# One-core transformer block with two expert mixtures: first mixture computed from held weights, first routing reordered

## What is computed

```python
y = attention(x, bias, mask, ...)            # 16 heads of 64, layer norms before and after
# first mixture: one expert of 8 for each token, at most ceil(T / 8 * 1.25) tokens to an expert, the others go to expert 0
final_e = _route(tokens, router_w)           # rank inside the expert by probability, ties by order
h = relu(tokens @ W1[e] + b1[e])             # 256 -> 1024
y = h @ W2[e] + b2[e]                        # 1024 -> 256
x = x + y
# second mixture: two experts of 8 for each token, and a shared part; then a gated layer of experts per sequence
x = x + gated(choice_mixture(x) + shared(x))
```

## Time and profile before

| | |
|---|---|
| median of 3 runs | 637.75 us |
| the profiled execution's own time | 638.58 us |
| its span, first to last instruction | 636.9 us |
| PE busy | 556.8 us, 87% of the span |
| DVE, ACT, GpSimd busy | 326.8, 247.3, 239.2 us |
| DMA | 80.05 MB, 126 GB/s mean |
| mean granted TensorE clock | 0.959 |

### The profile page before, as it was taken

One profiled execution on the slowest core, in us unless ns is written; L12 is line 12 of the kernel. 1 busy time (PEld: TensorE's weight loads), 2 busy tenths in 40 slices (PEclk: granted clock), 3 DMA queues, 4 the chain that ended last, 5 costly groups with the idle time before them and its releaser, 6 DMA issues.

```text
span 636.9 us, 11284 instructions
## 1 busy us (share of the span) xinstructions
PE 556.8 (87%) x3452; PEld 440.6 (69%) x3453; DVE 326.8 (51%) x973; ACT 247.3 (39%) x664; POOL 239.2 (38%) x392
## 2 busy tenths in 40 slices
PE   0599999662199999999999999999999989999895
PEld 0488888451056666666787897788888868777664
DVE  3477676459422222464253774444444425566665
ACT  0254454340022222222464433555565535444342
POOL 5322121000111112100482545565555427777860
PEclk9999999885599999999999999999999979999999
DMA  8940000039921101122347701565555623465662
GB/s 166 403 200 1 3 2 1 2 132 463 306 76 30 32 32 51 33 90 89 100 86 242 231 1 51 141 164 155 163 158 159 157 75 100 136 182 180 190 181 70
DMA packets 52222, 80.05 MB, mean 126 GB/s; under 512 B 11138, under 2 KB 43907, under 8 KB 51652
## 3 DMA queue, kind: packets, MB, share of 16 engines
q1 hardware_dynamic: 44004, 57.03, 26.1%
q0 software_dynamic: 8160, 22.29, 14.5%
HBM read 54.13 MB, written 25.17 MB: 125 GB/s over the span
## 4 chain that ended last, share of the span: by engine, by line
PE 76%; DVE 8%; DMA 4%; issue 4%; ACT 3%; POOL 3%; SPq 1%; another core or an unknown queue 0%; ACTq 0%; POOLq 0%; DVEq 0%
PE psum L1464 9%; PE psum L1383 9%; PE psum L1228 9%; PE psum L1246 8%; PE psum L1116 5%; PE psum L1478 5%; PE psum L1088 5%; PE psum L1393 4%; PE psum L1526 3%; PE psum L1456 3%; POOL arena L870 2%; PE psum L1238 2%; PE psum L1096 1%; PE psum L1411 1%; DMA arena<-x 1%
## 5 line engine op out<-in xcount | busy, mean ns | idle before, releaser
L870 POOL DMA_INDIRECT arena<-x,row_tok x72 | 69.3, 963 | 52.4 <-PE psum L1456 45.5
L870 POOL DMA_INDIRECT arena<-y_sorted,pos_k_i x64 | 63.7, 995 | 34.7 <-issue 15.3
L1464 PE MATMUL psum<-big_w,arena 128*128 x288 | 73.9, 379 | 0.0
L870 POOL DMA_INDIRECT arena<-h_late,row_tok x16 | 15.4, 960 | 145.6 <-PE psum L1220 84.8
L1383 PE MATMUL psum<-arena,big_w 128*128 128x256 f32 x256 | 62.5, 394 | 0.5 <-ACT arena L1816 0.5
L1526 PE MATMUL psum<-big_w,arena 128*128 x256 | 62.9, 379 | 0.0
L1228 PE MATMUL psum<-big_w,arena 128*128 x128 | 59.6, 609 | 0.8 <-DVE arena L2371 0.8
L1464 PEld LDWEIGHTS psum<-big_w,arena 128*128 128x128 f32 x288 | 54.5, 190 | 7.3
L1246 PE MATMUL psum<-arena 128*128 x256 | 58.0, 380 | 1.5 <-ACT arena L1729 1.5
L1383 PEld LDWEIGHTS psum<-arena,big_w 128*128 128x128 f32 x256 | 49.1, 199 | 8.5 <-ACT arena L1816 1.2
L1246 PEld LDWEIGHTS psum<-arena 128*128 128x128 f32 x256 | 47.5, 190 | 8.0 <-issue 2.2
(11 more groups left out here) (317 smaller groups left out, 1054.4 us busy)
## 6 DMA issues: line engine op xcount, KB each, us to landing
y_sorted<-arena SPq DMA_DIRECT2D x72, 128.0 KB
tokens<-x SPq DMA_DIRECT2D x4, 1024.0 KB, 22.2
x<-tokens SPq DMA_DIRECT2D x16, 256.0 KB, 3.0
z_kept<-arena SPq DMA_DIRECT2D x16, 256.0 KB
out<-arena SPq DMA_DIRECT2D x16, 256.0 KB
y_late<-arena SPq DMA_DIRECT2D x16, 128.0 KB, 1.7
big_w<-expert_w_t SPq DMA_DIRECT2D x1, 2048.0 KB, 8.1
arena<-x,row_tok POOLq DMA_INDIRECT x72
```

Source lines behind the costliest of these rows:

```text
L870: pool.indirect_dma_start(dst, None, rows, bass.IndirectOffsetOnAxis(ap=idx, axis=0)).then_inc(done, 16)
L1464: mm = pe.matmul(bank[2 + i % RT][:, 0:2 * M1], c_gt[i % RT][:, k, :], mgu_s[:, k, bass.ds(e, 1), :].rearrange("p a m -> p (a m)"), start= ...
```

## The change

Six edits:

- **Mixture.** `expert_up` holds W1 as the stationary operand (blocks of 128 x 128) and moves the 128 tokens: 16 matmuls of 128 columns whose result has the hidden units on the partitions. `turn_up`, `up_copy` and `act1` are gone; ACT's relu starts at half of expert_up (`up_half`), DVE's at its end; results and `act_t` alternate between two sets of buffers. The weights' place no longer depends on a register: tile i uses slot i mod 8 of `big_w`, and for tiles 8 to 15 SP loads the tile's W1 (1 MB, `load_w1`) when expert_up(i-8) is done. PE's loop is written out; it waits for the reloads before tiles 8 and 12.
- **Rows.** Seven tiles' variances, scaling and turning move ahead of the last projection on their engines; tile 7 alone follows it. The logits are computed in groups of 128 columns, the Exp table is loaded last.
- **Stores and loads.** SP stores seven tiles of `h_late` early, the last one apart. x is loaded after the table, the first gather and the two biases.
- **Comparisons.** ACT copies the spread keys to SBUF (`rows_s`), GpSimd makes "is less" for tiles 5, 6 and 7; tile 0's "is less or equal" is split in two.
- **Last tile.** DVE's relu of tile 15 precedes add_bias(14).
- **71 choice tiles** instead of 72; SP's store loop there is written out.

The diff, cut to its core (the general branch and plain renamings are left out):

```diff
-    TILES2 = -(-((2 * T + E1 * (P - 1)) // P) // RT) * RT
+    TILES2 = (2 * T + E1 * (P - 1)) // P
+act_t = [G.take(NF, P) for _ in range(2)]
+G.at += FF
...
+        sp.wait_ge(hnorm, NTW)
+        sp.dma_start(h_late[0:1, :], h_l[0:1, NTW, :]).then_inc(l_hs, 16)
+        sp.dma_start(late_rows[:, 0:NTW - 1, :], h_l[:, 0:NTW - 1, :]).then_inc(l_hs, 16)
         sp.wait_ge(hnorm, NTW + 1)
-        sp.dma_start(h_late[0:1, :], h_l[0:1, NTW, :]).then_inc(l_hs, 16)
-        sp.dma_start(h_late[1:, :].rearrange("(c p) d -> p c d", p=P), h_l[:, 0:NTW, :]).then_inc(l_hs, 16)
-        sp.wait_ge(l_ht, (NTW + 2) // 2)
-        sp.wait_ge(l_hs, 32)
+        sp.dma_start(late_rows[:, NTW - 1, :], h_l[:, NTW - 1, :]).then_inc(l_hs, 16)
         sp.dma_start(w2_s, w2.rearrange("p (e k d) -> p e k d", e=E0, k=NF)).then_inc(ld_w2, 16)
-        sp.wait_ge(l_lg, 1)
-        load_x()
     sp.wait_ge(table, 1)
     sp.wait_ge(got[0], 16)
     sp.dma_start(b1_s, b1).then_inc(ld_b, 16)
     sp.dma_start(b2_s, b2.rearrange("e d -> (e d)").partition_broadcast(P)
                  .rearrange("p (e d) -> p e d", e=E0)).then_inc(ld_b, 16)
+    load_x()
...
-        store_tile(0, 0)
-        with sp.Fori(0, E0 // 2 if late else (tiles - 1) // 2) as r:
-            for v in range(2):
+        def load_w1(i):
+            if i >= E0:
+                sp.wait_ge(up_ps, i - E0 + 1)
+            e = sp.value_load(tile_e[0:1, i:i + 1], min_val=0, max_val=E0 - 1)
+            sp.dma_start(w1_s[:, i % E0, :, :].rearrange("p k f -> p (k f)"),
+                         w1[:, bass.ds(e * (KD * FF), KD * FF)]).then_inc(w1_got[i // 4 % 2], 16)
...
+        for i in range(tiles - 1):
+            if i + E0 < tiles:
+                load_w1(i + E0)
+            store_tile(i, i % 2)
         sp.wait_ge(up_ps, tiles)
         load_shared()
...
+        pool.wait_ge(l_rows_ev, 2)
+        for m in range(NTW - NGB, NTW):
+            pool.tensor_scalar(beats[m][:, 0:(m + 1) * P], rows_s[:, 0:(m + 1) * P], key_l[:, m:m + 1], None, ALU.is_lt).then_inc(l_beat_g, 1)
...
             pe.wait_ge(l_beat, m + 1)
+            if m >= NTW - NGB:
+                pe.wait_ge(l_beat_g, m - NTW + NGB + 1)
...
-    def expert_up(i, e):
+    def expert_up(i):
+        u, at = i % 2, i % E0 * (KD * FF)
         pe.wait_ge(g_ev, i + 1)
-        pe.wait_ge(up_ev, i)
-        for k in range(KD):
-            for f in range(2):
-                mm = pe.matmul(bank[1 + f], g_t[:, k, :],
-                               big_w[:, bass.ds(e * (KD * FF) + (k * FF + f * 512), 512)],
+        if i >= 2:
+            pe.wait_ge(t_eva, i)
+            pe.wait_ge(t_evd, i)
+        for f in range(NF):
+            for k in range(KD):
+                c = at + k * FF + f * P
+                mm = pe.matmul(bank[1 + 2 * u + f // 4][:, (f % 4) * P:(f % 4 + 1) * P], big_w[:, c:c + P], g_t[:, k, :],
                                start=k == 0, stop=k == KD - 1)
+            if f == NF // 2 - 1:
+                mm.then_inc(up_half, 1)
         mm.then_inc(up_ps, 1)
...
-    def turn_up(j, u):
-        pe.wait_ge(up_ev, j + 1)
-        pe.wait_ge(t_eva, j + 1)
-        pe.wait_ge(t_evd, j + 1)
-        for f in range(NF):
-            mm = pe.transpose(bank[3 + f // 4][:, (f % 4) * P:(f % 4 + 1) * P], act1[u][:, f * P:(f + 1) * P], ident[:, :])
-        mm.then_inc(t_ps, 1)
...
-            mm = pe.matmul(bank[5 + u][:, 0:D], act_t[:, f, :], arena[:, bass.ds(e * (NF * D) + f * D, D)],
+            mm = pe.matmul(bank[5 + j % 2][:, 0:D], act_t[j % 2][:, f, :], arena[:, bass.ds(e * (NF * D) + f * D, D)],
...
+    def experts(tiles, late):
-        pe.wait_ge(ld_w1, 16)
-        pe.wait_ge(ld_w2, 16)
+        e = {i: i for i in range(E0)} if late else {}
+        if late:
+            pe.wait_ge(ld_w1, 16)
+        for i in range(tiles):
+            if i % 4 == 0 and (i >= E0 or not late):
+                n = 4 * (i // E0 + (0 if late else 1))
+                pe.wait_ge(w1_got[i // 4 % 2], 16 * (n - max(0, i + 4 - tiles)))
+            expert_up(i)
+            if i + 1 < tiles:
+                rows_in(i + 1, (i + 1) % 2, (i + 1) // 2)
+            if i == 1:
+                pe.wait_ge(ld_w2, 16)
+            if i:
+                expert_down(i - 1, e.pop(i - 1))
+            if i not in e and i % 2 == 0:
+                n = min(2, tiles - i)
+                e.update(zip(range(i, i + n), numbers(tile_e[0:1, i:i + n], n)))
+        expert_down(tiles - 1, e.pop(tiles - 1))
...
+        def turn_h(c, bk, at, n):
+            pe.wait_ge(hnorm, n)
+            for k in range(KD):
+                mm = pe.transpose(bk[:, (at * KD + k) * P:(at * KD + k + 1) * P], h_l[:, c, k * P:(k + 1) * P], ident[:, :])
+            return mm
+        def logits_of(cells):
+            for k in range(KD):
+                for c, g, n in cells:
+                    mm = pe.matmul(bank[7][32 * g:32 * g + 32, n * P:(n + 1) * P], router_g[:, k, :], ht_l[:, c, k * P:(k + 1) * P],
+                                   start=k == 0, stop=k == KD - 1)
+            return mm
+        for m in range(NTW // 2 - 1):
+            turn_h(2 * m, bank[m], 0, 2 * m + 1)
+            turn_h(2 * m + 1, bank[m], 1, 2 * m + 2).then_inc(l_ht, 1)
         project_late_rows(NTW - 1)
...
-        for g in range(NTW // 2):
-            pe.wait_ge(l_htc, g + 1)
-            for k in range(KD):
-                mm = pe.matmul(bank[6][32 * g:32 * g + 32, 0:2 * P], router_g[:, k, :], ht_l[:, 2 * g:2 * g + 2, k * P:(k + 1) * P],
-                               start=k == 0, stop=k == KD - 1)
-        mm.then_inc(lt_ps, 1)
+        turn_h(NTW, bank[3], 1, NTW - 1)
+        turn_h(NTW - 2, bank[3], 0, NTW).then_inc(l_ht, 1)
+        pe.wait_ge(l_htc, NTW // 2 - 1)
+        for n in range(2):
+            logits_of([(2 * g + n, g, n) for g in range(NTW // 2 - 1)])
+        pe.wait_ge(l_htc, NTW // 2)
+        logits_of([(NTW, NTW // 2 - 2, 2), (NTW - 2, NTW // 2 - 1, 0)]).then_inc(lt_ps, 1)
+        turn_h(NTW - 1, bank[5], 0, NTW + 1).then_inc(l_ht, 1)
         pe.wait_ge(l_htc, NTW // 2 + 1)
-        for k in range(KD):
-            pe.matmul(bank[7][:, 0:E0], ht_l[:, NTW, k * P:(k + 1) * P], router_g[:, k, 0:E0], start=k == 0, stop=k == KD - 1)
+        logits_of([(NTW - 1, NTW // 2 - 1, 1)]).then_inc(lt_ps, 1)
         pe.wait_ge(lt_ev, 1)
+        pe.transpose(bank[1][:, 0:32], lgt_s[64:96, 2 * P:3 * P], ident[64:96, 64:96])
+        pe.wait_ge(lt_ev, 2)
         for n in range(2):
-            mm = pe.transpose(bank[5][:, n * P:(n + 1) * P], lgt_s[:, n * P:(n + 1) * P], ident[:, :])
+            mm = pe.transpose(bank[0][:, n * P:(n + 1) * P], lgt_s[:, n * P:(n + 1) * P], ident[:, :])
...
+            act.copy(dst, src).then_inc(l_htc, 1)
+        act.activation(act_warm[:, :], eps_col[:, :], ACT.Sqrt)
+        late_rstd(1, 0, NTW + 1)
+        late_out(NTW - 2)
         late_values_summed(NTW - 1)
+        pair = [bank[m].rearrange("p (c d) -> p c d", c=2) for m in range(NTW // 2)]
+        for m in range(NTW // 2 - 1):
+            copy_h(m + 1, ht_l[:, 2 * m:2 * m + 2, :], pair[m])
+        act.copy(iota_l, iota_f[:, :].unsqueeze(2).broadcast_to([P, P, NTW])).then_inc(l_rep, 1)
         late_out(NTW - 1)
-        act.wait_ge(ovar, 1)
-        act.activation(rstd_l, mv_l[:, :, 1], ACT.Sqrt, bias=eps_col[:, 0:1]).then_inc(osd, 1)
+        copy_h(NTW // 2, ht_l[:, NTW - 2:NTW + 1:2, :], pair[NTW // 2 - 1])
+        late_rstd(3, NTW - 1, NTW)
+        copy_h(NTW // 2 + 1, ht_l[:, NTW - 1, :], bank[5][:, 0:D])
+        act.wait_ge(lt_ps, 1)
...
+        act.wait_ge(lt_ps, 2)
+        act.copy(lgt_s[:, 0:2 * P], bank[7][:, 0:2 * P]).then_inc(lt_ev, 1)
...
-        hold(act, t_ps, j + 1)
+        hold(act, up_half, j + 1)
         for f in range(NF // 2):
-            a = act.activation(act_t[:, f, :], bank[3][:, f * P:(f + 1) * P], ACT.Relu,
+            a = act.activation(act_t[u][:, f, :], bank[1 + 2 * u][:, f * P:(f + 1) * P], ACT.Relu,
                                bias=b1_s[:, bass.ds(e * NF + f, 1)])
         a.then_inc(t_eva, 1)
...
+        def scaled(c):
             dve.tensor_scalar(h_l[:, c, :], o_l[:, c, :], mv_l[:, c, 0:1], rstd_l[:, c:c + 1], ALU.subtract, ALU.mult).then_inc(hnorm, 1)
+        def row_variance(c, n):
+            late_stats(c).then_inc(gch0, 1)
+            dve.wait_ge(gch0, end + n)
+            dve.bn_aggr(mv_l[:, c, :], st_l[:, c, :]).then_inc(ovar, 1)
+        def inverse(c0, c1, n_sd, n):
+            dve.wait_ge(osd, n_sd)
+            dve.reciprocal(rstd_l[:, c0:c1], rstd_l[:, c0:c1]).then_inc(gch0, 1)
+            dve.wait_ge(gch0, end + n)
+        inverse(0, NTW + 1, 1, 1)
+        for c in range(NTW // 2):
+            scaled(c)
+        row_variance(NTW - 2, 2)
+        for c in (NTW - 4, NTW - 3, NTW):
+            scaled(c)
+        inverse(NTW - 2, NTW - 1, 2, 3)
+        scaled(NTW - 2)
+        row_variance(NTW - 1, 4)
+        inverse(NTW - 1, NTW, 3, 5)
+        scaled(NTW - 1)
...
```

(10 more changed lines are left out.)

153 lines of the change are left out of this document (59 added, 94 removed).

## The result

The changed kernel takes 615.68 us (median of 4 runs, 613.04 to 616.60); the kernel before took 637.83 beside it (637.45 to 641.01). The ratio is 0.9638, with a 95% interval of 0.9601 to 0.9675. Predicted were 617.0 us, in 612 to 625. The profiled execution took 616.07 us with a span of 614.3, against 638.58 and 636.9 before, so its span is 22.6 us shorter.

A forecast was written before the change was run, and what follows sets the result against it. PE's work and waits were taken to bound the kernel (76% of the chain that ended last). 4.5 + 3.3 + 2.9 + 10.3 - 1.9 + 1.6 = 20.7 us gain, from 637.75 to 617.0; range 612 to 625.

The forecast's parts named there:

- Rows, turning, logits: From the copy of the last projected rows to DVE's first read of logits: 9.15 us become 4.65, gain 4.5.
- the cover I named: Other eight tiles' work hides in DVE's free time before the last rows and PE's gap waiting for ACT (twelve transposes).
- Comparisons: DVE loses "is less" for tiles 5 to 7, gain 3.3 us; GpSimd's 6.3 us hide in 8.8 beside DVE.
- First gather: At the mixture's start, with x behind it, the gather lands in the median 3.4 us, not 6.3: gain 2.9.
- Mixture: First mixture: transposes go, expert_up takes 3.63 us, a tile 7.31 instead of 7.99: gain 10.3 us.
- Join: Behind the first mixture PE idles about 2.9 us and the clock falls: 1.9 us charged, bounds 0 and 1.9.
- its rival: The clock stays up behind the first mixture: 1.9 us back, 615.1 us; chance 0.10.
- Choice: Choice stage: one tile fewer, at 1.62 us from tile to tile, gain 1.6 us.

The follow-up runs named there:

- rows turned late: Changed kernel with the transposes of the first six normed tiles behind the last projection again and their copies behind ScalarE's last square root; 621.65 us.
- x ahead: Changed kernel with the four loads of x issued ahead of the table, after GpSimd's comparisons, not behind the first gather; 619.47 us.
- the run that undoes it: Changed kernel with only the mixture put back to its old form (4 matmuls of 512 columns, copy, 8 transposes, W1 resident); 626.48 us.
- the first of the filled runs: Changed kernel with shared weights loaded early, 12 constant matmuls ahead of the last but one projection and 12 behind the table's matmuls; 610.60 us.
- no reloads: Changed kernel without the eight reloads of W1 and PE's waits for them; tiles 8 to 15 use the weights of tiles 0 to 7; 615.65 us.
- 20 matmuls: Changed kernel with 20 matmuls of 128 columns on constants on PE between the table and the first gathered rows; 617.60 us.
- 72 tiles: Changed kernel with 72 choice tiles again instead of 71; 619.35 us.
- all on VectorE: Changed kernel with all comparisons made by VectorE again, none by GpSimd; 617.97 us.
- five on GpSimd: Changed kernel with GpSimd comparing tiles 3 to 7, 3840 columns instead of 2688; 616.55 us.
- second filled run: Changed kernel with shared weights loaded early, 12 constant matmuls ahead of the last but one projection, 10 ahead of the table's matmuls and 18 behind; 611.54 us.

## Why the prediction was right, step by step

**Rows, turning, logits: right.** 4.5 predicted, 4.6 found. The run with the rows turned late shows that the cover I named works: twelve transposes in an idle stretch of PE, three copies beside VectorE's statistics. I had left out that these transposes also keep PE busy ahead of the last projection.

**Comparisons: right, with the slack too large.** 3.3 in both. But GpSimd took 2.80 ns a column, not the 2.34 of its two-input operation. With 6.3 of the 8.8 us that I had counted, 2.5 would have been free; it took 7.53 of 9.53, from 138.19 to 147.72, and 2.0 were. The Trainium skill ("GPSIMD Engine Reference", Engine selection) holds one-input work on GpSimd to be at about line rate; VectorE's comparisons grow by 0.13 us for 128 columns, 1.03 ns a column, so here GpSimd is 2.7 times slower, and at five tiles it is the late one.

**First gather: right in cause, small in size.** From the median landing I expected 2.9 us; it was 3.5. The run with x ahead shows the cause: 3.8 us.

**Mixture: right, and its closeness is partly luck.** 10.3 predicted, 10.5 found, 10.0 in the run that undoes it, 11.2 by that run's profile. Errors in it cancel: expert_up takes 3.57 where the query projection gave 3.63 (a tile of 7.25, not 7.31: 0.9 us in 14 tiles), the second one took 3.84, and the first 6.35, not 5.6. I had carried over 5.6 with the words that it starts at the slow clock either way. How much of it runs at the slow clock depends on when the clock rises: in these runs the first expert_up took between 5.47 and 6.52, in the old form 5.59 and 6.36. I had also put the 3.84 of the earlier trace rows down to large loads. The second expert_up took 3.84 in the changed kernel, at 364 GB/s, and with x ahead, at 227; the third took 3.57 at 285 in the one and, in the first of the filled runs, at 366. So transfers don't explain it. What the second ones share is an idle time of 0.70 us ahead of them; that this is the cause wasn't tested.

**Join: the wrong step.** I charged 1.9 us for a falling clock behind a gap of 2.9. The gap was 3.4 and the clock stayed. It is not that the mechanism was wrong. Eight profiles have this code at the join, with PE idle for 3.1 to 4.1 us, the changed kernel's among them; in five (no reloads, 20 matmuls, x ahead, 72 tiles, turned late) the clock fell, in three (changed, all on VectorE, five on GpSimd) it did not. Where it fell it cost 1.6 to 2.6 us, read from the first transposes to the next. Five in eight by a mean of 2.0 is 1.2: that would have been the term, not 1.9 or 0. So neither my forecast nor its rival describes the code: with the same instructions at the join both outcomes occur. What decides it stays open; the length of the gap alone does not (3.32 and 3.37 without a fall, 3.14 and 3.33 with one). These are single profiles of eight kernels; that one and the same kernel does both from run to run is likely by them, and not shown. The Trainium skill ("TensorE: Matmul & The Clock Gate", Part 1) says that the chip looks at its own times, not the program's, so that the same kernel shows other counts of slow matmuls from run to run. These rows fit that, but none of the kernels was profiled twice.

**Choice: not contradicted, and not proven.** 2.2 us were found for 1.6. But over the eleven profiles with 71 tiles the stretch from the join to the last store, less what a fall at the join cost, runs from 206.9 to 210.8 us; the kernel before, with 72, had 210.1.

**Not in the sum:** the tail lost 0.9 us. PE is on much of its chain up to about 531 us; from there this runs mainly through GpSimd's gathers of y_sorted, one behind the other. The tail took 119.7 to 120.9 us in twelve of the thirteen profiles and 124.5 in the second filled run, without any edit to it.

The sum was 20.7 for 22.6. Join and choice together brought 2.5 us more than summed, the first gather and the logits 0.7, the mixture 0.2; the tail, the loads between bias and join, and the stretch up to the copy took 1.5 back. The time of 617.0 was 1.3 too high, well inside the range. Since the profiled execution is one without the fall, part of the 2.5 is an accident of that execution.

## What to carry to other kernels

Holding the weights in the array and moving the rows through it saves the transposes behind a layer, and costs nothing in weight loads where the trace already shows 128-column matmuls 113 ns apart. Find what is queued ahead of a late transfer on its issuing engine before charging the transfer: here an order on SP that the kernel before had covered cost 3.4 us once the cover was gone. And a clock that falls behind idle time belongs in a sum as a chance times a price, both from several profiles, and one profile with the fall and one without differ by it, whatever the edit. Filling the wait pays only if the fill, at the slow clock, still ends before the data is there.

## What the runs showed of the hardware that I had not expected

In these profiles the granted clock doesn't fall after a fixed idle time. An idle time of 2.99 us was followed by the fall in seven of eleven profiles, the kernel before and the changed one among them, and not in four; 1.39 us at the next wait were followed by it in the run with the rows turned late and not in the kernel before; 1.77 us were followed by it in the second filled run; 3.1 to 4.1 us at the join in five of eight. The rise isn't tied to the work alone either: the first expert_up of one code took 5.47 to 6.52 us, according to when the clock went from 0.50 (1.2 GHz) to 1.00 (2.4 GHz) within it.

GpSimd compares fp32 columns into bf16 at 2.80 to 2.84 ns each, without slowing VectorE's comparisons beside it (876 ns for 640 columns with it and without).

Reloads of 1 MB beside the matmuls cost these nothing that can be measured: 3.57 us with them and without. A first gather issued into 4 MB of x, on the other hand, is on PE 3.8 us later than without it.
